# Statistics, roots and scales of four of the ternary network's eight tiles moved beside the products of tiles 0 to 3

## The reference, cut to what matters

```
t = to_tokens(x)                         # x after the third block
u = ln_t(t)                              # mean and variance over 512 channels
xq = act_quant(rmsnorm(u))               # 127/max|.|, round, clip to [-32, 127]
gate, up = silu(xq @ w1q.T), xq @ w2q.T  # 512 -> 1408, weights in {-1, 0, 1}
h = gate * up
y = act_quant(rmsnorm(h)) @ w3q.T        # 1408 -> 512
t = t + y
```

## Time and profile before

| | |
|---|---|
| three runs, median | 1008.05 us (1004.0, 1008.05, 1008.83) |
| the profiled execution, own time | 1002.8 us |
| its span in the trace | 1000.9 us |
| busy, PE / DVE / ACT / POOL | 929.3 / 635.8 / 544.5 / 148.8 us |
| mean granted TensorE clock | 0.979 of full speed |
| the ternary network in the span | from 888.5 us to the end |

### The profile page before, as it was taken

The page is one execution under the profiler, slowest core; times in us unless marked ns, Lnnn a source line. Parts: engine busy times, 40 slices in busy tenths (PEclk is TensorE's granted clock), DMA queues, the critical chain, the costliest instruction groups (busy, mean ns, idle before and its releaser), DMA issues. The chain is left out here.

```text
span 1000.9 us, 21143 instructions
## 1 busy us (share of the span) xinstructions
PE 929.3 (93%) x7748; PEld 615.3 (61%) x7749; DVE 635.8 (64%) x1281; ACT 544.5 (54%) x857; POOL 148.8 (15%) x169
## 2 busy tenths in 40 slices
PE   5998996999999999999999999999999969966795
PEld 4545543677766666766687677668764448853453
DVE  5388695556754645754656665665656876677673
ACT  3685776456654555654556665656654213235674
POOL 0000102001220120220121122012106710002000
PEclk9999998999999999999999999999999989997999
DMA  8770646578776567676578857866896600000001
GB/s 285 273 244 2 254 153 197 206 218 275 244 247 220 179 225 229 215 252 220 178 248 262 272 198 236 256 199 241 272 272 206 184 13 1 2 0 1 1 22 63
DMA packets 164884, 181.77 MB, mean 182 GB/s; under 512 B 54610, under 2 KB 132434, under 8 KB 164851
## 3 DMA queue, kind: packets, MB, share of 16 engines
q1 hardware_dynamic: 152338, 147.35, 45.4%
q0 software_dynamic: 9808, 32.12, 9.7%
q10 hardware_dynamic: 2704, 1.87, 0.6%
HBM read 155.09 MB, written 14.68 MB: 170 GB/s over the span
## 5 line engine op out<-in xcount | busy, mean ns | idle before, releaser
L1094 DVE SCALAR_TENSOR_TENSOR w_lo<-raw_first,w_hi 128x1024 f16<-128x1024 f32 x144 | 172.6, 1219 | 53.3 <-ACT w_hi L585 53.3
L852 PE MATMUL pa<-x,w_hi 128*128 128x256 f16 (+2 forms) x576 | 171.3, 297 | 3.6 <-issue 2.5
L854 PE MATMUL pa<-x,w_lo 128*128 128x256 f16 (+2 forms) x576 | 171.3, 297 | 0.0
L853 PE MATMUL pa<-x,w_hi 128*128 128x256 f16 (+2 forms) x576 | 171.3, 297 | 0.0
L852 PE MATMUL pb<-x,w_hi 128*128 128x256 f16 (+2 forms) x576 | 170.6, 296 | 0.0
L853 PE MATMUL pb<-x,w_hi 128*128 128x256 f16 (+2 forms) x576 | 170.6, 296 | 0.0
L854 PE MATMUL pb<-x,w_lo 128*128 128x256 f16 (+2 forms) x576 | 170.6, 296 | 0.0
L1101 DVE SCALAR_TENSOR_TENSOR between<-pb,between 128x320 f32<-128x320 f32 (+1 forms) x144 | 73.9, 513 | 132.2 <-ACT between L589 132.2
L585 ACT ACTIVATE w_hi<-raw_first 128x1024 f16<-128x1024 f32 x144 | 147.8, 1050 | 15.1 <-PE pt L854 12.9
L1094 DVE SCALAR_TENSOR_TENSOR w_lo<-raw_last,w_hi 128x1024 f16<-128x1024 f32 x72 | 87.7, 1218 | 58.5 <-ACT w_hi L585 58.5
L593 ACT CAST early<-between 128x320 f16<-128x320 f32 (+1 forms) x144 | 68.4, 475 | 95.0 <-DVE between L1101 95.0
(11 more groups left out here) (282 smaller groups left out, 1619.3 us busy)
## 6 DMA issues: line engine op xcount, KB each, us to landing
raw_first<-in_gate_up SPq DMA_DIRECT2D x96, 512.0 KB, 5.0
raw_last<-in_gate_up SPq DMA_DIRECT2D x32, 512.0 KB, 3.8
raw_first<-in_down SPq DMA_DIRECT2D x32, 512.0 KB, 5.0
raw_last<-in_down SPq DMA_DIRECT2D x32, 512.0 KB, 3.6
chunks<-in_f SPq DMA_DIRECT2D x16, 704.0 KB, 5.5
slot_y<-chunks POOLq DMA_DIRECT2D x16, 512.0 KB, 3.2
chunks<-in_f SPq DMA_DIRECT2D x6, 768.0 KB, 4.5
raw_first<-in_sgate SPq DMA_DIRECT2D x6, 512.0 KB, 6.0
```

The source lines that it names most:

```text
L852: T.matmul(out, hi_a, hi_b, start=first, stop=False, **flags)
L853: T.matmul(out, hi_a, lo_b, start=False, stop=False, **flags)
L854: return T.matmul(out, lo_a, hi_b, start=False, stop=last, **flags)
L1094: V.scalar_tensor_tensor(w_lo[:, j % RING, c], raw[j % RING][:, c], W_SCALE, w_hi[:, j % RING, c], ALU.mult, ALU.subtract).then_inc(split_ ...
```

## The change

The front runs for tiles 0 to 3 only (with the roots in 4 columns), and the state of tiles 4 and 5 is still turned there. The rest is placed by the new function `beside(t, i)`, called on DVE after each part: additions of tiles 5 and 6 after (0,1) and (0,2), that of tile 7 after (1,0), statistics 4 to 7 after (1,1), (1,2), (2,0), (2,1), the roots of tiles 4 to 7 after (2,2), maxima 4 and 5 after (3,1), maxima 6 and 7 and the scales after (3,2). POOL makes `z` and rounds for all four of these tiles. `quant`, `turn_q` and `q_copy` of tiles 4 to 7 follow tile 3, the turns behind `second(1)`. The order of waits on shared banks is changed to suit.

```diff
-        QUANT_AFTER = {0: (4, 5), 1: (6, 7)}
-        TURN_AFTER = {0: (2, 3), 1: (4, 5), 2: (6, 7)}
+        QUANT_AFTER = {3: (4, 5, 6, 7)}
+        TURN_AFTER = {0: (2, 3), 3: (4, 5, 6, 7)}
+        Z_PARTS = [([0, 2], [1, 3]), ([], [4, 5, 6, 7])]
...
         def _(pool):
-            pool.wait_ge(rstd_ready, 1)
-            for t in range(1, NT, 2):
-                nc.gpsimd.tensor_scalar(z[:, t, :], x_tm[:, t, :], col(RSTD, t), col(SHIFT, t),
-                                        ALU.mult, ALU.add).then_inc(z_ready[1], 1)
-            for t in POOL_ZR:
-                scale_and_round(pool, nc.gpsimd, t, zr_ready[1])
+            for part in range(2):
+                pool.wait_ge(rstd_ready, part + 1)
+                for t in Z_PARTS[part][1]:
+                    nc.gpsimd.tensor_scalar(z[:, t, :], x_tm[:, t, :], col(RSTD, t), col(SHIFT, t),
+                                            ALU.mult, ALU.add).then_inc(z_ready[1], 1)
+                for t in POOL_ZR:
+                    if t // HALF_TILES == part:
+                        scale_and_round(pool, nc.gpsimd, t, zr_ready[1])
...
             act.wait_ge(rstd_ready, 1)
-            for t in range(0, NT, 2):
+            for t in Z_PARTS[0][0]:
...
-                for j in TURN_AFTER.get(t, ()):
-                    q_copy(j)
                 if t >= 4 and t % 2 == 0:
                     out_copy(t - 4)
...
                     square(t)
                     if t >= 5:
                         out_copy(t - 4)
+                for j in TURN_AFTER.get(t, ()):
+                    q_copy(j)
...
-            for t in range(NT):
+            def turn_state(t):
...
+            for t in range(HALF_TILES + 2):
+                turn_state(t)
...
             def turn_q(t):
                 pe.wait_ge(q_ready, t + 1)
                 if t >= 2:
                     pe.wait_ge(q_cm_ready, t - 1)
+                if t >= HALF_TILES:
+                    pe.wait_ge(h_cm_ready, 2 * 2)
...
             def turn_h(t):
                 pe.wait_ge(hq_ready, t + 1)
                 if t == 0:
+                    pe.wait_ge(q_cm_ready, HALF_TILES)
+                elif t == 2:
                     pe.wait_ge(q_cm_ready, NT)
-                else:
+                if t:
                     pe.wait_ge(h_cm_ready, 2 * t)
...
-                for j in TURN_AFTER.get(t, ()):
-                    turn_q(j)
+                if t == 0:
+                    turn_state(6)
+                if t == 1:
+                    turn_state(7)
...
                     second(t - 2)
+                for j in TURN_AFTER.get(t, ()):
+                    turn_q(j)
...
-            for t in range(NT):
+            def add_state(t):
                 dve.wait_ge(stack_turned, t + 1)
                 V.tensor_tensor(x_tm[:, t, :], (x_ps, y_ps)[t % 2][:, :], x_tm[:, t, :], ALU.add).then_inc(x3_ready, 1)
-                if t:
-                    stats(t - 1)
-            stats(NT - 1)
-            dve.wait_ge(dve_step, done[0])
...
+            def roots(part):
+                t0, t1 = part * HALF_TILES, (part + 1) * HALF_TILES
+                dve.wait_ge(dve_step, done[0])
+                for t in range(t0, t1):
+                    step(V.bn_aggr(mv[:, t, :], st[:, t, :]))
+                dve.wait_ge(dve_step, done[0])
+                rsqrt(nc, link, cols(RSTD, t0, t1), mv[:, t0:t1, 1], BOTH_SCALE, BOTH_EPS, scratch)
+                V.scalar_tensor_tensor(cols(SHIFT, t0, t1), mv[:, t0:t1, 0], -1.0, cols(RSTD, t0, t1),
+                                       ALU.mult, ALU.mult).then_inc(rstd_ready, 1)
+
+            add_state(0)
+            for t in range(1, HALF_TILES):
+                add_state(t)
+                stats(t - 1)
+            stats(HALF_TILES - 1)
+            roots(0)
+            add_state(4)
             for t in range(HALF_TILES):
                 z_max(t)
             q_scales(0)
             for t in range(HALF_TILES):
                 quant(t)
-            for t in range(HALF_TILES, NT):
-                z_max(t)
-            q_scales(1)
-            dve.wait_ge(dve_step, done[0])
+
+            def beside(t, i):
+                if t == 0 and i:
+                    add_state(4 + i)
+                if t == 1 and i == 0:
+                    add_state(7)
+                if t == 1 and i:
+                    stats(3 + i)
+                if t == 2 and i < 2:
+                    stats(6 + i)
+                if t == 2 and i == 2:
+                    roots(1)
+                if t == 3 and i:
+                    z_max(2 + 2 * i)
+                    z_max(3 + 2 * i)
+                if t == 3 and i == 2:
+                    q_scales(1)
...
                     if t % 2 and i == 0:
                         h_max(t - 1)
+                    beside(t, i)
```

More of the change, by code:

```diff
@@ L1914, in z_max @@
             def z_max(t):
-                dve.wait_ge(z_ready[t % 2], t // 2 + 1)
+                mine, ready = (ACT_ZR, z_ready[0]) if t in ACT_ZR else (POOL_ZR, z_ready[1])
+                dve.wait_ge(ready, mine.index(t) + 1)
                 step(V.tensor_reduce(col(ZMAX, t), z[:, t, :], AX.X, ALU.max, apply_absolute_value=True))
@@ L1947, in add_y @@
                                        ALU.mult, ALU.add).then_inc(x4_ready, 1)
-            for t in range(NT):
+            def add_state(t):
                 dve.wait_ge(stack_turned, t + 1)
                 V.tensor_tensor(x_tm[:, t, :], (x_ps, y_ps)[t % 2][:, :], x_tm[:, t, :], ALU.add).then_inc(x3_ready, 1)
-                if t:
-                    stats(t - 1)
-            stats(NT - 1)
-            dve.wait_ge(dve_step, done[0])
-            for t in range(NT):
-                step(V.bn_aggr(mv[:, t, :], st[:, t, :]))
-            dve.wait_ge(dve_step, done[0])
-            rsqrt(nc, link, cols(RSTD, 0, NT), mv[:, :, 1], BOTH_SCALE, BOTH_EPS, scratch)
-            V.scalar_tensor_tensor(cols(SHIFT, 0, NT), mv[:, :, 0], -1.0, cols(RSTD, 0, NT),
-                                   ALU.mult, ALU.mult).then_inc(rstd_ready, 1)
+            def roots(part):
[14 more added lines that the diff above has]
+            add_state(4)
             for t in range(HALF_TILES):
```

## The result

The changed kernel takes 1014.55 us (median of 6 runs, 1009.93 to 1017.58) against 1008.15 for the kernel before (6 runs). The ratio is 1.0066 with a 95% interval of 1.0042 to 1.0090: slower by 0.7%, some 6.6 us, where +7.25 was forecast.

A forecast was written before the change was run, and what follows sets the result against it. Bound taken as DVE alone at the front, then a loop of TensorE, ACT and DVE. -5.04 + 1.42 + 6.97 + 3.9 = +7.25 us on the median of 1008.05 gives 1015.3 us, range 1009.0 to 1020.0.

The forecast's parts named there:

- front: Work on DVE ahead of the first product: four addition and statistics pairs and half the aggregates leave, -5.04 us.
- tiles 0 and 1: From the first product to `h(2,0)`: state turn +0.44, wait of tile 7's addition +1.15, given back 0.17; +1.42 us.
- tiles 2 and 3: DVE from `h(2,0)` to `h_max(3)`: 11.17 us of added work and waits, 4.2 filled into holes; +6.97 us.
- behind tile 3: TensorE from `second(1)` to tile 4's first product: low clock +2.1 and four turns +1.8; +3.9 us.
- the pair's row: Profile row of POOL's two roundings beside DVE's quantisations: 1.63 us against 1.37 without, 0.26 more where one met quantisations.
- about 3 us: Sign that the forecast is right: DVE waits about 3 us for POOL ahead of `h_max(3)`.
- clock and turns cost little: Rival at `second(1)`: TensorE's clock not down, turns at their lower bound; +4.25 us, 1012.3 us, chance 0.17.
- TensorE sets tiles 2 and 3: Rival at `h_max(3)`: TensorE, not DVE, sets the pace; -4.6 us, 1003.4 us, not slower, chance 0.08.
- The low clock did not reach tile 4: Rival denied: pauses between turns keep 1.2 GHz in tile 4's first two parts; +10.65 us, 1018.7 us, chance 0.12.
- The front did get shorter: Rival denied: something other than DVE's statistics releases the first product, 5.04 gone; +12.3 us, 1020.3 us, chance 0.03.
- the first rival: The rival that clock and turns cost little at `second(1)`: +4.25 us, 1012.3 us, chance 0.17.

The follow-up runs named there:

- experiment 1: Changed kernel with the quantisations of tiles 4 to 7 moved behind `add_y(0)`; tile 4's first product at stage time 59.66 us against 64.13.
- experiment 2: Changed kernel with 34 unread matmuls keeping TensorE busy ahead of `second(1)`; tile 4's first product at stage time 61.72 us against 64.13.
- experiment 3: Changed kernel with the turns and copies of tiles 6 and 7 moved behind tile 4; tile 4's first product at stage time 63.23 us against 64.13.
- experiment 4: Changed kernel with each quantisation of tiles 4 to 7 held until GpSimd rounded all four; `h_max(3)` starts 4.12 us after the first rounding's start, against 3.91.
- experiment 7: Changed kernel with the quantisations of tiles 4 to 7 behind `add_y(0)`, timed against the kernel before: ratio 1.0032; tile 4's first product at 59.05 us.

## Why the prediction was right, point by point

| step | forecast | measured, stage times |
|---|---|---|
| front: first product | -5.04 | -5.23 (20.47 to 15.24) |
| tiles 0 and 1: to `h(2,0)` | +1.42 | +0.99 (40.33 to 36.09, less the front) |
| tiles 2 and 3: to `h_max(3)` | +6.97 | +7.22 (52.03 to 55.01, less the two above) |
| behind tile 3: to tile 4's first product | +3.9 | +4.33 |
| sum | +7.25 | +7.31 |

The mechanism was right at each step. That the sum came within 0.06 is luck: the steps miss by 0.19 to 0.43, two each way, and a stage time differed by 0.61 between two profiles of one kernel.

- *The front.* Four pairs of addition and statistics went as forecast, and the addition of tile 4 was hidden: DVE's wait for ACT's first `z` went from 0.88 to 0.28. The 0.19 over the forecast is within what executions differ by: in experiments 1 to 4 and 7, with the same front, the first product came at 15.26 to 15.63.
- *Tiles 0 and 1.* The wait of tile 7's addition came as said: 0.48, and `h(1,1)` 3.37 after `h(1,0)` (forecast 3.34). The step is 0.43 smaller, all of it in tile 0, because TensorE's clock rose earlier against its first product: the second part's first four matmuls took 1.17 in this profile and 1.52 in that of the kernel before. This 0.35 is luck, as they took 1.03 to 1.29 in the other profiles, and it paid for the turn in tile 0, which cost 0.36 (forecast 0.44).
- *Tiles 2 and 3.* The roots cost the 2.87 from 935.14 to 938.01 (forecast 3.0). GpSimd's roundings took 3.53 where 3.33 was put in: three of them are 0.26 longer beside a quantisation, not 0.2. That the two engines disturb each other is shown by experiment 4. By the rule of the Trainium skill's page "SBUF — State Buffer" ("Who interferes with whom"), which the prediction weighed, the later of a VectorE instruction in a two-port mode and a GpSimd instruction is blocked until the first has finished. By the trace neither was held for a whole instruction of the other's here: a rounding lost 0.26, and the quantisations kept their 0.43. The sum was nearer to the pair's row than to the rule. DVE's wait for POOL was 2.12 in four pieces, not "about 3 us", as quantisations stand between them.
- *Behind tile 3.* `second(1)` lost 2.32 (4.85 - 2.53, forecast 2.1), and experiment 2 got 2.41 back by keeping TensorE busy. The four turns took 2.06 (955.59 to 957.65, forecast 1.8); in experiment 2, at the full clock, they took 1.81 (956.73 to 958.54). So the excess of this step is the clock too, which cost 2.52 in all (6.70 - 4.18) where 2.1 was put in.

The rivals: that clock and turns cost little is out by experiment 2, for both. That TensorE sets tiles 2 and 3 is out by the 7.67 us wait on `add_y(0)` and by experiment 1. The low clock did not reach tile 4 (1.00 in its stretch). The front did get shorter. What experiment 3 adds: two turns cost as much behind tile 4 as behind tile 3, since by tile 6 a kernel with two turns moved is 0.17 ahead, 0.15 of which it had before them. On the first rival the prediction says that no row shows a wait of just 7 us. A shorter one already spoke against the rival: in the kernel before, soon behind the 3.9 us wait of the earlier trace rows, tile 3's first four matmuls took 1.79, where 1.03 is usual at the full clock:

```profile
932.95 1.79 PE L1862 MATMUL g<-ternary,q_cm 128*128 128x512 fp8e4 x4
```

## What to carry to other kernels

Work taken off a front is only hidden if each piece stands in a wait that the timeline shows on its engine, and if nothing that another engine waits for is queued behind it: the same pieces gave +0.7% in one order and -0.4% in another. Look above all at what stands ahead of the instruction that releases TensorE; a long wait there is paid twice, once as time and once as a slower clock behind it (`second(1)` ran slower behind 3.84 and 7.67 us here, and not behind 0.87 and 1.37). And compare single profiles from the first instruction of the changed stage, not from the span's start: counted from there, the stage's own start moved by up to 8 us here.

## What was not expected of the hardware

After waits of equal length TensorE's clock was not the same from one execution to the next. Experiment 1 waited 3.84 us ahead of `second(1)` in both of its profiles, and the 11 matmuls took 4.85 us in one and 3.86 in the other. Tile 2's last part stands behind a wait of 3.70 us in the changed kernel and in experiment 1, and its first four matmuls took 1.46 in one and 0.82 in the other; that moved the `h` of this part by some 0.2 us. And a rounding of GpSimd that overlapped a quantisation of DVE took some 0.26 us longer, though by the trace it had started first, ahead of the quantisation at 945.38. The second rounding in the changed kernel, beside the 0.69 of one of experiment 4's undisturbed four (2.73 in all):

```profile
945.33 0.95 POOL L1707 TENSOR_SCALAR z<-z,stat 128x512 f32<-128x512 f32 x1
```
